# Flamingo block on one core: the feed-forward part starts three unit tiles of the next batch between the two phases of a batch

## What is computed

```python
x = x + tanh(g_xattn) * attention(ctx, layernorm(x), mask, ...)
x = x + tanh(g_ffn)   * ffn(layernorm(x))

def ffn(x):                                    # 512 -> 2048 hidden units -> 512
    h = einsum('bsd,hd->bsh', act_quant(x), weight_quant(w1))
    h = silu(depthwise_conv1d(h, conv_w, conv_b))      # 3 taps along the 1024 tokens
    return einsum('bsd,hd->bsh', act_quant(h), weight_quant(w2))
```

## Time and profile before

| | us |
|---|---|
| Median of 3 runs (1778.56 to 1781.55) | 1779.76 |
| The profiled execution's own time | 1780.23 |
| Its span in the profile | 1778.5 |
| PE busy, DVE busy in the span | 1649.8, 1133.4 |
| ACT busy, POOL busy in the span | 836.4, 718.6 |

### The profile page before, as it was taken

One profiled execution on the slowest core, in us unless ns is written; L12 is line 12 of the kernel. 1 busy time (PEld: TensorE's weight loads), 2 busy tenths in 40 slices (PEclk: granted clock), 3 DMA queues, 4 the chain that ended last, 5 costly groups with the idle time before them and its releaser, 6 DMA issues. The chain is left out here.

```text
span 1778.5 us, 23983 instructions
## 1 busy us (share of the span) xinstructions
PE 1649.8 (93%) x8754; PEld 1013.2 (57%) x8754; DVE 1133.4 (64%) x2183; ACT 836.4 (47%) x901; POOL 718.6 (40%) x314
## 2 busy tenths in 40 slices
PE   6999999999998999999999999999998796987868
PEld 5788788888875544454445444454455443544434
DVE  7777634444327677657865687668538749399792
ACT  4132323222210444424563456335647777787776
POOL 1221000000000688756885677657925225062250
PEclk9899999999999999999999999999999898998989
DMA  7687555444442422202231213212234020020201
GB/s 264 247 273 251 199 179 195 165 166 161 158 160 107 144 84 85 84 2 108 73 127 64 108 61 108 84 66 79 73 118 142 24 95 21 15 85 1 95 1 48
DMA packets 108583, 200.87 MB, mean 113 GB/s; under 512 B 8384, under 2 KB 33984, under 8 KB 108480
## 3 DMA queue, kind: packets, MB, share of 16 engines
q1 hardware_dynamic: 108480, 199.49, 32.0%
HBM read 124.75 MB, written 74.71 MB: 112 GB/s over the span
## 5 line engine op out<-in xcount | busy, mean ns | idle before, releaser
L748 POOL TENSOR_TENSOR acc<-acc,pr 128x1024 f32<-128x1024 f32 x188 | 448.8, 2387 | 130.5 <-ACT pr L780 113.9
L780 ACT ACTIVATE pr<-ps,mcol 128x1024 f32<-128x1024 f32 x256 | 284.2, 1114 | 363.0 <-PE ps L1520 360.1
L1062 DVE CUSTOM_DVE_ANT_0 junk<-ps,mbias 128x512 bf16<-128x512 f32 x512 | 333.0, 688 | 128.4 <-PE ps L1495 123.8
L1532 PE MATMUL ps<-pr,vv 128*64 128x512 f32 x1024 | 274.7, 618 | 0.0
L755 POOL TENSOR_TENSOR h_first<-h_first,last_tap 128x1023 f32<-128x1023 f32 x44 | 103.6, 2356 | 252.9 <-DVE h_first L1409 223.2
L729 POOL MEMSET nmt<- 128x128 f32 x1 | 0.2, 205 | 343.2 <-DVE chl L1293 343.2
L1495 PE MATMUL ps<-kh,qh 64*128 64x512 f32 x512 | 122.7, 450 | 11.0 <-DVE nmv L1062 9.9
L1602 PE MATMUL ps<-xiT,w1q 128*128 128x512 bf16 x512 | 120.2, 380 | 10.7 <-ACT xiT L770 5.0
L748 POOL TENSOR_TENSOR acc<-pr 128x1024 f32<-128x1024 f32 x32 | 76.9, 2402 | 121.4 <-ACT pr L780 121.4
L1495 PEld LDWEIGHTS ps<-kh,qh 64*128 64x128 f32 x512 | 50.8, 184 | 128.8 <-issue 99.3
L1766 PE MATMUL ps<-w2q,hq 128*128 128x512 bf16 x512 | 121.4, 391 | 1.0 <-ACT hq L973 0.8
(11 more groups left out here) (175 smaller groups left out, 3147.5 us busy)
## 6 DMA issues: line engine op xcount, KB each, us to landing
craw<-in_ctxT SPq DMA_DIRECT2D x8, 2048.0 KB, 8.6
xa<-in_x SPq DMA_DIRECT2D x32, 256.0 KB, 3.9
wraw<-in_w1T SPq DMA_DIRECT2D x16, 512.0 KB, 6.0
wraw<-in_w2T SPq DMA_DIRECT2D x16, 512.0 KB, 7.0
q_split<-kqh SPq DMA_DIRECT2D x32, 256.0 KB, 2.0
q_split<-kql SPq DMA_DIRECT2D x32, 256.0 KB, 2.4
base<-lna SPq DMA_DIRECT2D x32, 256.0 KB, 4.1
k_split<-kqh SPq DMA_DIRECT2D x32, 256.0 KB, 2.0
```

Of the source, the lines that this page charges most:

```text
L748: nc.gpsimd.tensor_tensor(acc[:, blk % 2, :], first, pr[:, (8 * blk + j) % NP, :], ALU.add).then_inc(pool_acc, 1)
L780: act.activation(pr[:, u % NP, :], ps[:, 2 * (u % 2):2 * (u % 2) + 2, :].rearrange("p a t -> p (a t)"), ACT.Exp, bias=mcol[:, (u // 64) * ...
L1062: dve.tensor_tensor_reduce(out=(junk1 if n < LEAD and n % 2 else junk)[:, e, :], in0=ps[:, first_bank(n) + e, :], in1=mbias[:, b % 2, kk * ...
L1532: last = pe.matmul(ps[64 * e:64 * e + 64, 6 + blk % 2, :], vv[g % 2][:, j, 64 * e:64 * e + 64], pr[:, u % NP, e * CH:(e + 1) * CH], start= ...
```

## The change

Seven things are done to the feed-forward part.

1. The first three unit tiles of batch b+1 are computed during the last tiles of phase one and the beginning of phase two of batch b. All names of progress counts now carry the batch.
2. The turned inputs `xiT` and the scales `row` have two copies, and are prepared one batch earlier: batch 1's between the attention's last projections, batch 2's in phase two of batch 0, batch 3's in phase two of batch 1.
3. Batch 3's layer norm moves with them: its first five steps to phase two of batch 0, the last three to phase two of batch 1.
4. The fourth unit tile's `pe_first` and the first tile's transposes of batch b+1 stand on PE in front of the product of tile 7 of batch b.
5. Bank pairs are reassigned by batch (`PAIR`), so that the three early tiles have banks that phase two doesn't use yet.
6. x2 has four tiles of 128 tokens, loaded and stored tile by tile.
7. GpSimd's loop over batches is written out.

```diff
+        PAIR = [[j % 3 for j in range(KH)]]
+        for b in range(1, B):
+            first_three = PAIR[b - 1][KH - 3:]
+            PAIR.append([first_three[j] if j < 3 else first_three[(j - 4) % 3] for j in range(KH)])
+        def out_bank(b, i):
+            return 2 * PAIR[b][KH - 3] + i % 2
+        def turned_bank(b, i):
+            return 2 * PAIR[b][KH - 2] if i % 2 else 6
+        def norm_bank(b):
+            return 2 if b == 0 else 6 if b == 1 else 2 * PAIR[b - 2][KH - 1]
...
 # SP
-                sp.wait_ge(dve_d, (b + 1) * D_DVE_N)
-                sp.dma_start(out[b * S:(b + 1) * S, :].rearrange("(j p) d -> p j d", p=P), x2[:]).then_inc(sp_out, 16)
+            for n in range(B * NT):
+                sp.wait_ge(dve_d, D_DVE[f"o{n // NT}_{n % NT}"])
+                sp.dma_start(out[n * P:(n + 1) * P, :], x2[:, n % RING, :]).then_inc(sp_out[n % RING], 16)
+                if 1 <= n <= B * NT - RING:
+                    sp.wait_ge(sp_out[(n - 1) % RING], 16 * ((n - 1) // RING + 1))
+                    load_x2(n - 1 + RING)
...
 # ACT
+            taps(0, 0)
+            taps(0, 1)
+            act_ln_row(act, 1)
+            for u in range(NT // 2):
+                act_ln_turned(act, 1, u)
+            for b in range(B):
                 for j in range(KH):
+                    if j + 2 >= KH and b + 1 < B:
+                        taps(b + 1, j + 2 - KH)
+                    elif j + 2 < KH and (b == 0 or j + 2 >= 3):
+                        taps(b, j + 2)
                     act.wait_ge(pe_ct, b * KH + j + 1)
                     act.activation(hT[:, :, j * P:(j + 1) * P], ps[:, 6:8, :]..., ACT.Silu).then_inc(act_d, 1)
+                if b + 1 < B:
+                    taps(b + 1, 2)
+                integers(b, 0)
...
+                    turned_units(b, i)
+                    if b == 0 and i == 1:
+                        act_ln_std(act, B - 1)
+                    if b + 2 < B and i == 4:
+                        act_ln_row(act, b + 2)
+                    if b + 2 < B and i in (5, 6):
+                        act_ln_turned(act, b + 2, 2 * (i - 5))
+                        act_ln_turned(act, b + 2, 2 * (i - 5) + 1)
...
 # DVE
+            norm_steps = ln_steps(dve, B - 1)
+            for b in range(B):
+                for j in range(KH):
+                    if b == 0 or j >= 3:
+                        first_tap(b, j)
+                    if j >= 2:
+                        biggest(b, j - 2)
+                    if j + 2 >= KH and b + 1 < B:
+                        dve_scaled(dve, b + 1, j + 2 - KH)
+                    elif j + 2 < KH and (b == 0 or j + 2 >= 4):
+                        dve_scaled(dve, b, j + 2)
...
                 for i in range(NT):
                     if i + 3 < NT:
+                        round_up(b, i + 3)
+                    if b == 0 and i in (0, 2, 3):
+                        norm_steps[2 + i - i // 2]()
+                    if b == 1 and i < 3:
+                        norm_steps[5 + i]()
+                    if i == NT - 1 and b + 1 < B:
+                        dve_scaled(dve, b + 1, 3)
+                    add_out(b, i)
...
 # PE, behind the attention's last products (project)
+                if i == 5:
+                    ln_row(pe, 1)
+                if i in (6, 7):
+                    ln_turn(pe, 1, 2 * (i - 6))
+                    ln_turn(pe, 1, 2 * (i - 6) + 1)
 # PE, pe_first(b, j), the waits of the batches behind the first
+            elif b and j < 3:
+                pe.wait_ge(dve_d, D_DVE[f"c{b - 1}_{KH - 3 + j}"])
+                pe.wait_ge(act_d, D_ACT[f"u{b - 1}_{KH - 3 + j}"])
+            elif b and j == 3:
+                pe.wait_ge(dve_d, D_DVE[f"c{b}_2"])
+                if b + 1 < B:
+                    pe.wait_ge(act_ln, (b + 1) * LN_ACT_N + LN_ACT_N)
+            elif b and j == 4:
+                pe.wait_ge(dve_d, D_DVE[f"o{b - 1}_{NT - 1}"])
+            elif b:
+                pe.wait_ge(act_d, D_ACT[f"hT{b - 1}_{NT - 1}"])
```

More of the change, by code:

```diff
@@ L421, in flamingo_gated_block @@
         LN_ACT, LN_ACT_N = counts(["row"] + [f"xT{i}" for i in range(NT // 2)])
[L422 to L432, removed]
+        names = ["g0_0", "g0_1"]
@@ L932, in _ @@
             c_act(act)
[L934 to L959, removed]
@@ new lines, in _ @@
+                for i in range(1, NT):
+                    if i + 1 < NT:
+                        integers(b, i + 1)
+                    turned_units(b, i)
[6 more added lines that the diff above has]
+                        act_ln_turned(act, b + 2, 2 * (i - 5) + 1)
@@ new lines, in done, with first_tap, biggest @@
+            def done(name):
+                dve.wait_ge(dve_d, D_DVE[name])
+            def first_tap(b, j):
+                done(f"g{b}_{j}")
+                dve.wait_ge(act_d, D_ACT[f"u{b}_{j}"])
+                units = h[tile(b, j)]
+                dve.scalar_tensor_tensor(out=units[:, 1:S], in0=pair(b, j)[:, 0:S - 1], scalar=convw[:, j, 0:1], in1=units[:, 1:S],
+                                         op0=ALU.mult, op1=ALU.add).then_inc(dve_d, 1)
+            def biggest(b, j):
+                dve.wait_ge(act_d, D_ACT[f"silu{b}_{j}"])
+                dve.tensor_reduce(hmax[:, j, :], hT[:, :, j * P:(j + 1) * P], AX.X, ALU.max, apply_absolute_value=True).then_inc(dve_d, 1)
@@ new lines, in turn_units @@
+            def turn_units(b, j):
+                pe.wait_ge(pool_tap, b * KH + j + 1)
+                if j:
+                    pe.wait_ge(act_d, D_ACT[f"silu{b}_{j - 1}"])
+                elif b:
+                    pe.wait_ge(act_d, D_ACT[f"hT{b - 1}_{NT - 2}"])
+                else:
+                    pe.wait_ge(act_ln, 2 * LN_ACT_N)
+                for i in range(NT):
+                    last = pe.transpose(ps[:, 6 + i // 4, (i % 4) * P:(i % 4 + 1) * P], h[tile(b, j)][:, i * P:(i + 1) * P], ident[:])
+                last.then_inc(pe_ct, 1)
@@ new lines, in second @@
+            def second(b, i):
+                pe.wait_ge(act_d, D_ACT[f"hT{b}_{i}" if i else f"hT{b}_0a"])
+                if i >= 2:
+                    pe.wait_ge(dve_d, D_DVE[f"o{b}_{i - 2}"])
+                elif b + 1 < B:
+                    pe.wait_ge(dve_d, D_DVE[f"c{b + 1}_0"])
+                for j in range(KH):
+                    if i == 0 and j == KH // 2:
+                        turn_h(b, 1)
+                        pe.wait_ge(act_d, D_ACT[f"hT{b}_0"])
+                    last = pe.matmul(ps[:, out_bank(b, i), :], hq[:, i % 2, j, :], w2q[:, j, :], start=j == 0, stop=j == KH - 1)
+                last.then_inc(pe_o, 1)
@@ L1754, in ffn @@
+            pe.wait_ge(dve_free5, use5["y", B - 1, NT - 1] + 1)
+            pe_first(pe, 0, 2)
+            for b in range(B):
+                for j in range(KH):
+                    if j + 3 >= KH and b + 1 < B:
+                        pe_first(pe, b + 1, j + 3 - KH)
+                    elif j + 3 < KH and (b == 0 or j + 3 >= 4):
+                        pe_first(pe, b, j + 3)
+                    if b == 0 or j:
+                        turn_units(b, j)
+                turn_h(b, 0)
                 if b == 0:
```

350 lines of the change are left out of this document (184 added, 166 removed).

## The result

The changed kernel takes 1751.37 us (median of 4 runs, 1750.98 to 1753.35), the kernel before 1780.12 (median of 4, 1778.56 to 1781.55; the 1779.76 further up is that of the first three): a ratio of 0.9843, with a 95% interval from 0.983 to 0.9855. The forecast was 1753, with a range from 1745 to 1766.

A forecast was written before the change was run, and what follows sets the result against it. VectorE was taken to bound phase one (3.45 us a tile), TensorE phase two (4.35), with gaps between. Terms chained batch by batch ended at 1751.6, 26.9 below 1778.5: 1753 us forecast from a 1779.76 median, range 1745 to 1766.

The forecast's parts named there:

- The ramp, O to F: Addition of tile 7 (O) to next batch's first tap of tile 15 (F): 45.3 us, last batch 44.3; before, over 55.
- The tail, F to A: First tap of tile 15 (F) to ScalarE's first integers (A): 10.1 us instead of 10.8, early-tile work filling idle VectorE time.
- The rival in which the moved tiles push: End of phase one: early tiles lengthen the path, 6.5 us at each of three boundaries, 1772 us; chance 0.12.
- A to P: ScalarE's first integers (A) to the product of tile 1 (P): 9.9 us in each batch, ScalarE's own chain.
- P to O: Product of tile 1 (P) to addition of tile 7 (O): 35.0, 35.0, 31.5, 28.85 us by batch, without batch 0's stall.
- The norm of batch 3, in batch 0: Phase two of batch 0: the norm's steps on VectorE delay the product of tile 2, a stall of 5.3 us.
- The rival in which the norm is hidden: Phase two of batch 0: statistics don't delay rounding 3, so no stall and no half clock, 1746 us; chance 0.12.
- The blocking by GpSimd: Norm in batch 0: `diag` on VectorE waits for GpSimd's addition; without such blocking it is done 1.2 us earlier.
- The clock behind the stall: Batch 0, phase two: idle for over 4 us, TensorE falls to half clock once more, costing 1.4 us, bounds 0 and 3.4.
- The rival in which the clock stays low: Batch 0, behind the stall: TensorE's half clock does not end once products run; chance 0.03 for the clock.
- Start, loads and stores: Preparations before the feed-forward part +2.7 us, rescaling at tile 14 +1.0; no load waits; end 3.2 behind last addition, was 8.6.
- The sum: All terms chained over the four batches: end of the span at 1751.6 us, 26.9 below 1778.5.

The follow-up runs named there:

- x1: The changed kernel with the first three unit tiles (and the fourth's `pe_first` and first tile's transposes) back in their own batch: 1767.68 us, 0.9936 of before.
- x7: The changed kernel with one unused maximum more on VectorE behind `biggest` of tile 14 in every batch: 1753.32 us, 0.9861 of before.
- x2: The changed kernel with diagonal and statistics of batch 3's norm spread over later tiles of batch 0, root at tile 3: 1745.55 us, 0.9813 of before.
- x3: The changed kernel with unread products added on TensorE at the boundaries between phases, to keep its clock up: 1748.22 us, 0.9834 of before.
- x6: The changed kernel with only `diag` moved, from ahead of the statistics to behind the rounding of tile 4 in batch 0: 1748.05 us, 0.982 of before.
- x8: The changed kernel with both later norm statistics and unread products keeping TensorE busy between phases: 1744.5 us, 0.9804 of before.
- x4: The kernel before, with only the last batch's output stored tile by tile: 1773.88 us, 0.9973 of before.

## Why the prediction was right, and which term was off

**What bounds.** Right. Phase one is VectorE's at 3.45 us a tile and phase two TensorE's at 4.35, before and after; what the change removed lay between them.

**The ramp, O to F.** Right to a tenth: 45.26, 45.26, 44.25 for 45.3, 45.3, 44.3. x1 shows it to be the early tiles' work: without them 54.1 to 55.2. "Over 55" for before was 56.9: it leaves out the first rescaling itself, about 1.2, but no term of the sum rests on it.

**The tail, F to A.** Right, 10.1. x7 shows the reason too: VectorE's seven instructions are the path, and one more costs its full length. The margin of 0.2 us was there: silu of tile 15 ended at 1401.47 (1400.45 + 1.02), and the last maximum started at 1401.67. The rival in which the moved tiles push, 1772, did not come.

**A to P.** Mis-sized a little: 9.9 forecast, 10.46, 10.62, 9.63 and 9.5 measured. The prediction let "falls to half clock as now" stand for the same price. The half clock lies elsewhere now (from 1401.9 to 1412.1 in batch 0), and over the whole first half product: 3.57 for 8 matmuls, where the earlier trace rows had 3.16. That is 0.6 in batch 0 and 0.7 in batch 1, and given back in part in the last two. In batch 0 it cost nothing in the end, as the stall behind it was that much shorter.

**P to O.** The preparations were sized right: 35.02 and 31.51 in batches 1 and 2 for 35.0 and 31.5, and 35.02 in batch 0 once x2 had removed the stall.

**The norm of batch 3, in batch 0.** Right in kind and place, mis-sized: 3.1 us for 5.3. This is the term that failed, and in it the last link, "table load, root, integers and copy to the product 5.21". Up to the aggregates the chain held: R, the first rounding, is at 1404.12, `diag` was to end at R + 8.5 and ended at 1412.42, R + 8.3; the aggregates were to end at R + 15.1 and ended at 1418.91, R + 14.8. From there to the product it was 3.95, not 5.21. The 1.28 us of the table load are missing in it, because the load ran at 1414.84, and ScalarE then waited for data. In the earlier trace rows it stood behind the aggregates only by coincidence: ScalarE had been busy with a copy until 1630.43, and the aggregates ended at 1630.44. The remainder is P itself, 0.6 late by the half clock, so that the product was due later. In sum: 5.3 - 1.3 - 0.3 - 0.6 = 3.1. No experiment moved the load on purpose. The kernel after, x1, x3, x6 and x7 have it start ahead of the end of the aggregates, each time within 0.02 us of the copy before it; in x2 and x8, where ScalarE had other work until then, it stands behind them, as in the earlier trace rows. The rival in which the norm is hidden did not come either: the stall and the half clock cost 4.6, and only the order of x2 and x8 hides it.

The Trainium skill, ScalarE: Activation LUTs, section What ACT_TABLE_LOAD costs, gives some 1283 ns for the load and a drain of some 1380 ns on top. The first agrees with the 1.28 us of these rows. Of the second the rows show nothing: in x2 the copy before the load ends at 1420.40, the load runs from 1420.42 to 1421.70, and the root starts at 1421.71. So 1.28 is the price here.

**The blocking by GpSimd.** Confirmed and sized by x6: 2.1 us for a diagonal of 1.22. The taps beside it take 3.33 and 3.35 us, and 2.35 alone. In batches 1 and 2 the third rounding pays the same (2.19 for 1.28) and it costs nothing there, with P to O at its bare sum. The Trainium skill, SBUF — State Buffer, section Who interferes with whom, says so of two SBUF inputs, as `diag` has. It also says that a VectorE instruction with at most one SBUF input, outside the modes with both ports, does not contend with GpSimd. The statistics have one, and the tap of 2.35 beside them in x6 agrees.

**The clock behind the stall.** Forecast 1.4, bounds 0 and 3.4; measured 1.44 (P to O of 39.60, less 35.02 and 3.14), with a stretch of 3.4 us at 0.50. The rival in which the clock stays low did not come: from the end of that stretch to the next boundary the clock was full.

**Start, loads and stores.** S to the first unit tile grew by 2.68 us (forecast 2.7), S to A by 3.08 (forecast 3.1). Additions never waited for a load. Stores of 256 KB landed in 2.0 us (median of 32). The end came at O + 3.3 for O + 3.2, and x4 gave the same alone.

**The sum.** End forecast 1751.6, measured 1749.3. Of the 2.3, 1.1 is S, which stood earlier by the stages ahead; 2.1 the stall; against them 0.7 of A to P over the batches (1.3 in the first two, 0.6 back in the last two), and roundings of 0.2. The mechanisms are as forecast; that the S of this execution helped by 1.1 is luck.

## What to carry to other kernels

When two phases are bound by different engines, the gap between them is where work is free: count the idle time of the engine that sets the next phase, move that much of the next batch into it, and then ask, as x7 did, whether one instruction more already costs. Work that the moved tiles now run beside (here GpSimd's taps beside the norm's diagonal) must be costed again, and steps with slack, as the norm's statistics, be spread over tiles rather than set in one block ahead of the pipeline's fill. And the last store of a kernel is on the path in full: stored by tiles, its last 256 KB end 3.3 us behind the last addition, where 2 MB took 8.6.

## What the runs showed of the hardware

- A table load does not wait for the data of the activation behind it. In the kernel after it ran at 1414.84, and the root at 1418.94, when its data came. Here the load of 1.28 us was hidden in that wait.
- VectorE and GpSimd block each other in turn, by whole instructions. Tap 1 (3.33) pays for a rounding begun 0.16 us ahead of it, `diag` (2.19) waits for tap 1, tap 2 (3.35) waits for `diag`: each begins its work as the other ends. The statistics beside tap 2 in x6 did not do this (2.35).
- The price of a dropped clock differs where the code is the same. A to P of batch 2, the same instructions in each, was 9.63 in the kernel after, 10.51 in x2, 10.43 in x6 and 10.34 in x7. It went by where the half-clock stretch ended against the first half product: in the kernel after it ended 5.0, 5.6, 7.2 and 7.6 us behind A where A to P was 9.54, 9.63, 10.46 and 10.62, and in the kernel before 5.0, 6.0, 6.2 and 6.4 us behind A for 9.54, 9.86, 9.96 and 10.04. The forecast's single 9.9 could not be better than about half a us for that reason.
- S, behind identical code, moved between 1307.7 and 1310.7 us. What made these 3 us stays open. They are as large as most effects that were separated here, so only marks inside one profile tell them apart.
